# Attention denominators: one TensorE group for four steps in place of two, on rotating PSUM banks

## The reference, cut to what matters

```python
x = h_t                                            # [8, 1024, 256]
xn = layernorm(x)
# attention A: 8 heads, low-rank keys (c_kv) and queries (c_q), rotary part of 32
attnA = softmax(q @ k.T * (128 + 32) ** -0.5) @ v_c
# attention B: 16 heads of 16; tokens fall in two classes by a cosine with g_info;
# a token attends to its own class (and 5 register tokens, which average both)
attnB = softmax(where(mask, q * 16 ** -0.5 @ k.T, -inf)) @ v
out = x + attnA @ W_O + b_O + attnB @ W_proj + b_proj
```

## Time and profile before

| | |
|---|---|
| median of 3 runs | 3112.72 us (3109.84 to 3118.35) |
| the profiled execution | 3124.31 us, its span 3122.5 us |
| busy: TensorE, VectorE, ScalarE, GpSimd | 2950.3, 2243.7, 1738.0, 896.3 us |
| denominators' matmuls on TensorE | 135.1 us busy, 1024 records |
| additions on GpSimd | 585.3 us busy, 128 instructions |

### The profile page before, as it was taken

How to read it: one execution, slowest core, us unless ns; L and a number is a source line. 1 busy time by engine, 2 the same in 40 slices (tenths; PEclk the granted TensorE clock), 3 DMA queues, 4 the chain that set the end, 5 groups by cost and what they waited for, 6 DMA issues and landing times.

```text
span 3122.5 us, 45726 instructions
## 1 busy us (share of the span) xinstructions
PE 2950.3 (94%) x17346; PEld 1304.0 (42%) x17346; DVE 2243.7 (72%) x4016; ACT 1738.0 (56%) x2047; POOL 896.3 (29%) x359
## 2 busy tenths in 40 slices
PE   7899989999999999999999999999999999999997
PEld 5555533334433344344433443344333443344333
DVE  5566625798669866887678767986688767876791
ACT  2333345665457645665566555764566556654574
POOL 3322226102530054004500252016400450035201
PEclk9999989999999999999999999999999999999998
DMA  5755354225011420234021501152023402160001
GB/s 195 229 204 186 136 162 73 56 47 109 19 35 47 80 61 23 62 59 85 20 65 37 107 20 45 37 90 57 20 61 56 86 19 68 35 109 17 20 14 36
DMA packets 128411, 225.01 MB, mean 72 GB/s; under 512 B 48546, under 2 KB 79170, under 8 KB 126000
## 3 DMA queue, kind: packets, MB, share of 16 engines
q1 hardware_dynamic: 128192, 222.10, 29.4%
HBM read 143.44 MB, written 78.32 MB: 71 GB/s over the span
## 4 chain that ended last, share of the span: by engine, by line
PE 71%; DVE 22%; issue 2%; ACT 2%; DMA 2%; POOL 1%; SPq 1%; POOLq 0%; ACTq 0%; DVEq 0%
PE O L1209 22%; DVE mx L1502 18%; PE M L1128 14%; PE M L1122 8%; PE S L1188 5%; PE S L1191 4%; PE M L1225 4%; PE M L1080 3%; PE M L1168 2%; PE M L1170 2%; PE M L1141 1%; PE M L1098 1%; ACT PT L975 1%; PE M L1094 1%; POOL SUM L846 1%
## 5 line engine op out<-in xcount | busy, mean ns | idle before, releaser
L1502 DVE TENSOR_REDUCE mx<-M 128x1 f32<-128x512 f32 x3037 | 1940.2, 684 | 535.3 <-PE M L1128 334.7
L975 ACT ACTIVATE PTx<-S 128x1024 f32<-128x1024 f32 x768 | 746.3, 1022 | 504.1 <-PE S L1191 289.0
L975 ACT ACTIVATE PT<-S 128x1024 f32<-128x1024 f32 x768 | 748.0, 1022 | 472.2 <-PE S L1191 240.4
L1128 PE MATMUL M<-KB,QB 50*128 50x512 f32 x2048 | 726.3, 487 | 73.0 <-DVE mx L1502 44.3
L1128 PEld LDWEIGHTS M<-KB,QB 50*128 50x128 f32 x2048 | 295.8, 186 | 780.2 <-DVE mx L1502 571.6
L1191 PE MATMUL S<-QB,KB 52*128 52x512 f32 x2048 | 454.1, 417 | 2.5 <-ACT PT L975 1.6
L1122 PE MATMUL M<-KA,QA 98*128 98x512 f32 x989 | 414.2, 460 | 15.7 <-DVE mx L1502 10.0
L846 POOL TENSOR_TENSOR SUM<-PT 128x2048 f32<-128x2048 f32 x64 | 292.8, 4574 | 397.7 <-PE M L1225 184.0
L846 POOL TENSOR_TENSOR SUM<-PTx 128x2048 f32<-128x2048 f32 x64 | 292.5, 4570 | 177.2 <-PE M L1225 177.2
L1188 PE MATMUL S<-QA,KA 114*128 114x512 f32 x1024 | 318.8, 415 | 3.8 <-DMA QA<-sh_d 3.4
L1122 PEld LDWEIGHTS M<-KA,QA 98*128 98x128 f32 x989 | 168.3, 188 | 308.4 <-issue 179.3
(11 more groups left out here) (199 smaller groups left out, 1887.4 us busy)
## 6 DMA issues: line engine op xcount, KB each, us to landing
KA<-kt_d SPq DMA_DIRECT2D x48, 512.0 KB, 7.1
QB<-qk_d SPq DMA_DIRECT2D x192, 128.0 KB
KB<-qk_d SPq DMA_DIRECT2D x192, 128.0 KB
qk_d<-QB SPq DMA_DIRECT2D x16, 1024.0 KB, 4.1
kt_d<-QB SPq DMA_DIRECT2D x16, 1024.0 KB, 4.3
RB<-recb_d SPq DMA_DIRECT2D x64, 256.0 KB
vb_d<-VB SPq DMA_DIRECT2D x8, 1536.0 KB, 5.5
VB<-vb_d SPq DMA_DIRECT2D x8, 1536.0 KB, 12.7
```

What stands on the lines that cost most here:

```text
L975: nc.scalar.activation(probs(k)[:, 2 * pair:2 * pair + 2, :], Sg[pair][:, :].rearrange("p (j s) -> p j s", j=2), ACT.Exp, scale=SCALE_A if ...
L1128: done = mm(m[:, :], QB[rows, 2 * q + a, at:at + P], KB[rows, 2 * q + a, keys], start=True, stop=True)
L1502: v.tensor_reduce(mx[:, g % 2, unit, kh:kh + 1], m[:, :], AX.X, ALU.max).then_inc(free, 1)
```

## The change

- GpSimd adds four steps' exponentials in place of two: `add_four` is called for t = 1, 2, 3; the first call adds two steps into one of two `SUM` buffers, the second and third add one more step each in place. That is three additions for four steps, and not two. The second and third wait for the one before.
- TensorE has one denominators group for four steps, as a job `dn` at the end of step 4i+7 (the last one of a stage at step 3 of B). It isn't accumulated over a head group: each goes to its own bank, in turn with the other jobs, and ScalarE copies it to a half of `DEN` (`take_dens`, at every fourth step).
- `DN` is gone, so jobs take turns on three banks in all steps but the `rv` ones of B.
- SP moves both halves of a head group (`den_d` with one dimension more, `RC` too), and VectorE adds the halves before the reciprocal, which stands at step 7 of the next group in place of 5.
- The last `po` jobs stand at steps 13 to 16 and not 12 to 15. `load_residual(b, 1)` moves to the end of the B stage, ahead of `recs` of group 6 and behind the store of the first half, and the residual addition to the end of GpSimd's B stage.

```diff
-PAIRS = STEPS_A // 2
+QUADS = STEPS_A // 4
...
+    s[3][3].append(("dn", QUADS - 1))
...
+    for i in range(QUADS - 1):
+        s[4 * i + 7][3].append(("dn", i))
     if not first:
-        for c, at in enumerate((12, 13, 14, 15)):
+        for c, at in enumerate((13, 14, 15, 16)):
...
-        of = 3 if three is not None and k >= three and not RV_AT <= k < RV_AT + NC // 2 else 2
+        of = 2 if len(slots) == STEPS_B and RV_AT <= k < RV_AT + NC // 2 else 3
...
-    SUM = sb("SUM", [P, 4, HALF])
+    SUM = sb("SUM", [P, 2, 4, HALF])
+    DEN = sb("DEN", [P, 2, HALF])
...
             if kind == "a":
-                wait_apart(sp, dn_free, n * GA + (g + 1))
-                src = RB[0:P:32, slot, :]
+                for i in (2 * g, 2 * g + 1):
+                    spot = dn_spot(n, i)
+                    wait_apart(sp, m_free[spot.bank], spot.upto())
+                sp.dma_start(den_d[slot].rearrange("w h s -> h w s"), DEN[0:P:32, :, :]).then_inc(den_out, 16)
+                wait_apart(sp, den_out, at * 16 + 16)
+                sp.dma_start(RC[:, slot, :, :], den_d[slot].rearrange("w h (r c) -> (h r) w c", c=16)
+                             ).then_inc(rc_in, 16)
...
             for g in range(GA):
-                if before and g == 0:
-                    load_residual(b, 1)
...
                     store_out(b, 0, [b_spot(b, last, ("po", c)) for c in range(4)])
-                    if last:
-                        load_residual(b, 1)
+                    load_residual(b, 1)
...
+        def add_four(n, i, t):
+
+            k, done = 4 * i + t, n * (3 * QUADS) + 3 * i
+            four = SUM[:, i % 2]
+            if t == 1:
+                if n or i >= 2:
+                    spot = dn_spot(n, i - 2) if i >= 2 else dn_spot(n - 1, QUADS - 2 + i)
+                    wait_apart(pool, m_full[spot.bank], spot.upto())
+            else:
+                wait_apart(pool, summed, done + t - 1)
             wait_apart(pool, e_done, n * (2 * STEPS) + (2 * k + 2))
-            nc.gpsimd.tensor_tensor(SUM[:, :, :], probs(k - 1), probs(k), ALU.add).then_inc(summed, 1)
+            nc.gpsimd.tensor_tensor(four, probs(k - 1) if t == 1 else four, probs(k), ALU.add).then_inc(summed, 1)
...
-            for i in range(PAIRS):
-                g, at = i // 4, i % 4
-                add_pair(n, i)
+            for i in range(QUADS):
+                add_four(n, i, 1)
+                if i % 2 == 0:
+                    if i >= 4:
+                        scale(n, "a", i // 2 - 2)
                     elif before:
-                        scale(b, "b", GB - 2 + g)
-                if before and i == 1:
-                    residual(b, 1)
+                        scale(b, "b", GB - 2 + i // 2)
+                add_four(n, i, 2)
+                add_four(n, i, 3)
...
+            residual(b, 1)
...
                 if 4 <= k < STEPS_A + 4:
-                    act.wait_ge(summed, n * PAIRS + ((k - 4) // 2 + 1))
+                    j = k - 4
+                    act.wait_ge(summed, n * (3 * QUADS) + (3 * (j // 4) + max(0, j % 4 - 1) + 1))
...
-            act.wait_ge(dn_done, n * PAIRS + 4 * (g + 1))
+            act.wait_ge(m_full[spot.bank], spot.upto())
+            nc.scalar.activation(DEN[:, i % 2, :], M4[spot.bank][:, :], ACT.Copy).then_inc(m_free[spot.bank], 1)
...
+            elif kind == "dn":
+                i = j[1]
+                pe.wait_ge(summed, n * (3 * QUADS) + (3 * i + 3))
+                for jj in range(4):
+                    done = mm(m[32 * jj:32 * jj + 32, :], ones32[:, :], SUM[:, i % 2, jj, :], start=True, stop=True,
+                              skip_group_check=True)
...
-                if k >= 3 and k % 2 == 1:
-                    denominators(n, b, (k - 3) // 2)
...
-            v.reciprocal(RC[:, g % 2, :], RC[:, g % 2, :]).then_inc(rc_done, 1)
+            of = RC[:, g % 2, 0, :]
+            if kind == "a":
+                own.link(v.tensor_tensor(of, of, RC[:, g % 2, 1, :], ALU.add))
+                own.settle()
+            v.reciprocal(of, of).then_inc(rc_done, 1)
```

More of the change, by code:

```diff
@@ L175, in jobs_a, with banks @@
     return s
-def banks(slots, three):
+def banks(slots):
     out = []
     for k, step in enumerate(slots):
-        of = 3 if three is not None and k >= three and not RV_AT <= k < RV_AT + NC // 2 else 2
+        of = 2 if len(slots) == STEPS_B and RV_AT <= k < RV_AT + NC // 2 else 3
         out += [(j, of) for part in step for j in part if j[0] != "rv" or j[1] == 0]
@@ L208 @@
 JOBS_B, JOBS_LAST = jobs_b(True), jobs_b(False)
-AT_A0, R0 = index(banks(JOBS_A0, None), U_PASS)
-AT_B, U_B = index(banks(JOBS_B, THREE), R0)
-AT_A, U_A = index(banks(JOBS_A, None), U_B)
+AT_A0, R0 = index(banks(JOBS_A0), U_PASS)
+AT_B, U_B = index(banks(JOBS_B), R0)
+AT_A, U_A = index(banks(JOBS_A), U_B)
 LOOP = less(U_A, R0)
 R1 = tuple(x + (B - 1) * y for x, y in zip(R0, LOOP))
-AT_LAST, U_LAST = index(banks(JOBS_LAST, THREE), R1)
-AT_TAIL, _ = index([(j, 2) for j in TAIL], U_LAST)
+AT_LAST, U_LAST = index(banks(JOBS_LAST), R1)
+AT_TAIL, _ = index([(j, 3) for j in TAIL], U_LAST)
 class Spot:
@@ L900, in _ @@
         b_steps(B - 1, True)
-        residual(B - 1, 1)
         scale(B - 1, "b", GB - 2)
@@ L993, in take_out, with take_dens @@
                 nc.scalar.activation(OB[:, q // 2, cols], O[:, :], ACT.Copy).then_inc(o_free, 1)
-        def take_dens(n, g):
-            act.wait_ge(dn_done, n * PAIRS + 4 * (g + 1))
-            if not (n == 0 and g < 2):
-                act.wait_ge(o_done, n * GROUPS + (g - 1))
-            nc.scalar.activation(RB[:, g % 2, :], DN[:, :], ACT.Copy).then_inc(dn_free, 1)
+        def take_dens(n, i):
+            spot, at = dn_spot(n, i), n * GROUPS + i // 2
+            if i % 2 == 0 and (n or i):
+                last = at - 1 if i else (n - 1) * GROUPS + (GA - 1)
+                act.wait_ge(den_out, last * 16 + 16)
+            act.wait_ge(m_full[spot.bank], spot.upto())
+            nc.scalar.activation(DEN[:, i % 2, :], M4[spot.bank][:, :], ACT.Copy).then_inc(m_free[spot.bank], 1)
         def a_steps(n, b, before):
@@ L1008, in a_steps @@
                     take_out(n, "a", k // NC - 1)
-                if k > NC and k % NC == 1:
-                    take_dens(n, k // NC - 1)
+                if k >= 7 and k % 4 == 3:
+                    take_dens(n, (k - 7) // 4)
         def b_steps(b, last):
@@ L1018, in b_steps @@
                     take_out(b, "b", k // NC - 1)
[L1019 to L1020 removed]
+                if k == 3:
+                    take_dens(b, QUADS - 1)
                 if k in (RS_AT, RS_AT + 1):
@@ L1106, in job @@
                 pass
-            elif spot.bank == 2 and spot.fixed in (R0[2], R1[2]):
-                pe.wait_ge(dn_free, b * GA + GA)
             elif not (spot.b is None and spot.fixed == 0):
@@ L1211, in values @@
             last.then_inc(pv_done, 1)
-        def denominators(n, b, i):
-            g, c = i // 4, i % 4
-            if c == 0:
-                if g == 0 and b is not None:
-                    pe.wait_ge(m_free[2], b * LOOP[2] + U_B[2])
-                elif g == 0:
-                    pe.wait_ge(m_free[2], U_PASS[2])
-                else:
-                    pe.wait_ge(dn_free, n * GA + g)
-            pe.wait_ge(summed, n * PAIRS + (i + 1))
-            for jj in range(4):
-                last = mm(DN[32 * jj:32 * jj + 32, :], ones32[:, :], SUM[:, jj, :],
-                          start=(c == 0), stop=(c == 3), skip_group_check=True)
-            last.then_inc(dn_done, 1)
         def of_batch(j, n, b):
-            own = j[0] in ("mb", "rs", "rt", "rv", "po") or (j[0] == "fa" and j[1] == "b")
+            own = j[0] in ("mb", "dn", "rs", "rt", "rv", "po") or (j[0] == "fa" and j[1] == "b")
             return b if own else n
@@ L1296, in b_steps @@
                     values(b, STEPS_A - 1, "a")
-                if k == 1:
-                    denominators(b, b, PAIRS - 1)
                 some(k, 3)
@@ L1494, in job @@
             kind = j[0]
-            if kind in ("rs", "rt") or (kind == "rv" and j[1] + 1 < NC):
+            if kind in ("dn", "rs", "rt") or (kind == "rv" and j[1] + 1 < NC):
                 return
@@ L1570, in a_steps @@
                     job(j, a_spot(n, b, j), b if j[0] == "po" else n, b)
-                if k % NC == 5:
-                    if k >= NC:
-                        invert(n, "a", k // NC - 1)
-                    elif before:
-                        invert(b, "b", GB - 1)
+                if k == 5 and before:
+                    invert(b, "b", GB - 1)
+                if k >= 15 and k % NC == 7:
+                    invert(n, "a", k // NC - 1)
         def b_steps(b, last):
@@ L1589, in b_steps @@
                     registers(b, last, k - RX_AT)
-                if k % NC == 5:
-                    invert(b, *(("b", k // NC - 1) if k >= NC else ("a", GA - 1)))
+                if k == 7:
+                    invert(b, "a", GA - 1)
```

(4 more changed lines are left out.)

38 lines of the change are left out of this document (15 added, 23 removed).

## The result

| | before | after |
|---|---|---|
| median | 3112.8 us (3109.8 to 3118.4) | 3079.3 us (3076.9 to 3086.7) |
| profiled execution: its span | 3122.5 us | 3084.9 us |
| busy: TensorE, VectorE, ScalarE, GpSimd | 2950.3, 2243.7, 1738.0, 896.3 us | 2881.6, 2302.6, 1750.9, 1185.5 us |

The ratio is 0.9894, 95% interval 0.9871 to 0.9917: faster by 1.1%. The forecast was 3011 us, with 2975 to 3075 as its range, so about a third of the forecast gain came and the time lies just over the range. In the profiles the gain is 37.6 us of span, where 102 were forecast; some of it is scatter, since the profiled execution before took 3124.3 us, 11.5 over its median.

What follows compares the result with a forecast made beforehand. TensorE bounds the A stages now, GpSimd after: stretch 119.8 + 2.5 + 1 = 123.3 us against 137.6, about 100 over seven stages, plus 2 in the first. 102 off the median gives 3011 us; own range 2990 to 3035, wider range 2975 to 3075.

Steps and rivals of the forecast that it cites:

- The rest at nothing: Small edits, among them eight ScalarE copies and four VectorE additions a stage, cost nothing, covered by idle time.
- if that cover went: Bound should ScalarE's and VectorE's idle time not hide the small copies and additions: 6.6 us a stage.
- the paragraph on contention: VectorE's four new additions could hold GpSimd up, at most 2.7 us a stage, giving 3030; no sign seen in trace.
- GpSimd takes TensorE's place as the bound: In A stages, 24 additions of 4.57 us, hand-overs and scalings sum to 119.8 us on GpSimd, against TensorE's 119.
- stretch: From an A stage's first addition to the exponential of step 35, in the next B stage: 137.6 us before, 123.3 forecast.
- TensorE's savings: In the stretch, fewer denominators groups save 7.7 us, the third bank 3 and 7: TensorE alone 119 us, 112 to 129.
- The moved residual: Loading XR behind the output store starts an A stage's first addition 2.5 us late, bounds 0 and 8.
- The first stage: First A stage, which ends on loads for the B stage: gain 2 us, bounds 0 and 6.
- The clock rival: TensorE idles a fifth of the time in second halves, its clock falls, half the gain is lost: 3061 us, chance 0.12.
- The loads late: XR comes 8 us late and not 2.5, so a stage gains 8.8 us: 3049 us, chance 0.12.
- No change: GpSimd's in-place addition with hand-over costs 5.2 us, not 4.6 to 4.85, taking 14 us a stage; chance 0.05.
- Slower: The clock stays down in the A stages' second halves, the stretch becomes 141 us: 3135 us, chance 0.08.

Runs made afterwards that it cites:

- reduction kernel: The changed kernel with VectorE adding the two halves by a one-operand tensor_reduce in place of the two-operand addition: 3023.5 us, 0.9716.
- control: The kernel before with an unused one-operand reduction of 16 columns ahead of each of A's 32 reciprocals on VectorE: 3116.0 us, 0.9997.

## Why the prediction was wrong, and what of it was right

| span of the profiled execution, difference to before | forecast | after | reduction kernel |
|---|---|---|---|
| seven later stages, steps 0 to 36 | -100 | 7 x (141.3 - 149.3) = -56.0 | 7 x (134.4 - 149.3) = -104.3 |
| first stage | -2 | +9.4 | +2.7 |
| before the first stage | 0 | +2.8 | +2.7 |
| all else | 0 | +6.2 | -0.9 |
| sum | -102 | -37.6 | -99.8 |

The table is of single executions, and that of the kernel before was a long one. In the control's trace, which is the same kernel with 32 cheap reductions more, steps 0 to 36 take 147.8 us and not 149.3, so some 10 us of both gains are scatter: by the medians they are 33.5 and 89. That of the reduction kernel is 12 us short of the 102 forecast.

**The step that failed** is "The rest at nothing", its "Four 128x16 additions on VectorE, each under a maximum's 0.68 us". Each of the three in a stage takes up to 3.66 us. Their work is 0.17 us; the rest is the GpSimd instruction that happens to run. The miss is the price of a single term: the reduction in its place brings the kernel from 3079.3 to 3023.5 us. That is 56 us of the 68 between forecast and result. The bound given, 6.6 us a stage "if that cover went", was for all small edits together and would have been 46 us; it was kept out of the sum, because the rows had no addition of two SBUF operands on VectorE and the nearest row that was taken, a maximum, reads one, from PSUM. That 6.6 lies so near to the 6.9 us a stage that the holds cost (141.3 - 134.4) is luck: it counts a length of 0.68 us for each addition, and more than half of it is ScalarE's copies.

The forecast came close to it, in the paragraph on contention, and took the wrong side: it let GpSimd be held up for the length of VectorE's short instruction, and found no sign of it in GpSimd's lengths. Those do stay at 4.57 us: it is the short instruction that waits for the long one. The trace of the kernel before has no sign of it either: in the stages no VectorE instruction with two operands in SBUF stands beside a GpSimd one, and the 12 of the first pass that stand beside a GpSimd `tensor_scalar` aren't held, as shown below. The Trainium skill (SBUF — State Buffer, Who interferes with whom) says that a VectorE instruction with two SBUF inputs and a GpSimd instruction that reads SBUF exclude each other, whoever issued first holding the shared ports for its whole length, and that one SBUF input doesn't contend. The traces agree for GpSimd's additions, and on the single input: the hold ends 0.03 to 0.04 us behind the addition, and the reduction's 0.19 us never grew. A GpSimd instruction held by VectorE is in none of these runs. By that rule the price could have been had from a row of the kernel before, as an estimate: up to 4.57 us each, 2.3 us in the mean, three times a stage (2.7 measured).

For another GpSimd instruction that reads SBUF the traces don't bear the rule out. In the first pass of the kernel before, a VectorE product of two operands in SBUF stands wholly inside a GpSimd `tensor_scalar`, which has one tensor to read (timelines of GpSimd and VectorE):

```profile
136.64 1.22 POOL L813 TENSOR_SCALAR PTx<-PT,early 128x256 f32<-128x256 f32 x1
...
137.02 0.45 DVE L1405 TENSOR_TENSOR early<-early 128x256 f32<-128x256 f32 x1
```

The twelve traces have 144 such VectorE instructions that start while a `tensor_scalar` runs. None of them takes over 0.47 us, and 0.40 to 0.43 is what their kind takes with GpSimd idle; the 96 that are held in these runs all stand beside an addition of two operands. Whether GpSimd's second operand, its operation or its length makes the difference was not tried.

**GpSimd takes TensorE's place as the bound: right.** 24 additions of 4.57 us, hand-overs of 0.27 us, the additions of a stage over 119.1 us after the first starts in the reduction kernel (119.8 forecast). Shortening the chain gave 63 us more, so it was the bound. With the later start the reduction kernel's stretch is 119.6 + 2.9 = 122.5 us, where 123.3 were forecast.

**TensorE's savings: right, a little low.** With most of GpSimd's third additions gone the forecast's stretch is 115.7 us (113.1 and 2.6 of later start), where 119 were summed for TensorE. Steps 0 to 36 take 127.9 us there with three banks, and 144.0 with two and all additions. The bank is thus worth up to 16 us a stage to TensorE, where 10 were summed ("bounds 0 and 7" and "0 and 10"), and 9.6 to the kernel, since GpSimd stops it there. The denominators' 7.7 us were not tried alone; nearest to it is the kernel with two banks, 4 us a stage under the control (144.0 and 147.8), the later start included.

**The moved residual: right** in time (sum 3 us late, 2.5 forecast) and in sign. It is no gain either way: 2.4 us of GpSimd in the stage or ahead of it.

**The first stage: wrong**, -2 forecast and +9.4 measured. The loads were named, but the step read their effect off the end of the stage ("the stage ends on them") and not off the small transfers in the same queue, of which `DEN` is now one and blocks ScalarE. The bounds, 0 and 6, had no loss in them. In the reduction kernel 2.7 us of loss are left; spread loads turn it into a gain of 5.

**The clock rival: right in what happens, not in why.** Its fall does come in the later halves, but behind the 2.7 us for which the held VectorE kept TensorE waiting. The mean granted clock is 0.977 before, 0.962 after and 0.981 with the reduction, where GpSimd is the bound just as well; over steps 0 to 36 of the seven later stages it is 0.981, 0.948 and 0.986. So "TensorE will idle there for a fifth of the time" isn't what brings it down. How much of the 56 us is the wait itself and how much the clock behind it was not separated: the held additions of the 24 places sum to 66 us, most of the first two of each stage under GpSimd's chain, and both went together in every run.

**The other rivals.** The loads late (3049), by 8 us: no, 3 us. No change (3113), on additions of over 5.2 us: no. Slower (3135): no. The rise before the first stage, 2.8 us, is within what the traces differ by: the first exponential of the stage starts at 427.2 to 430.2 us in the twelve of them, and at 429.1 and 429.2 in the two that add an instruction to the kernel before. The 6 us in the B stages of the changed kernel were not traced further; they are gone with the reduction.

Of what was to show it: GpSimd over 90% busy, idle 0.27 us, exponentials released by SUM and the residual last before the stage, all seen. TensorE busy near 85%: no, 94% in batch 1's stage, partly at the low clock, and 96% in the reduction kernel, as a busy TensorE includes matmuls stretched by their waits. "VectorE waiting for RC" was listed as a sign of trouble; it was the right tile, but the trouble stood in the busy time of its instruction and in no wait.

## What to carry to other kernels

Before a small operation is put on VectorE beside long GpSimd additions of two operands, count its operands in SBUF. With two of them it costs up to the longest GpSimd instruction and not its own length; with one in PSUM, or written as a reduction over both halves, it costs what it should. Ask then where each hold falls: one that another engine's chain covers costs little, one at the end of that chain costs more than its length. When an engine has a group whose mean is far above its shortest, compare the end of each with the end of what runs on the engine beside it: a wait of this kind shows as busy time, and neither the waits nor the idle column has it.

Where a move makes a queue's small transfer feed a copy that stands in the order of the exponentials, price the loads that stand ahead of it in the queue.

## What the runs showed of the hardware that was not expected

- VectorE's 128x16 addition of two SBUF operands takes 0.17 us with GpSimd idle and up to 3.66 us (3.79 in the kernel before with such additions) with a 4.57 us addition running; it ends 0.03 to 0.04 us after that one. It slips in between two GpSimd instructions that follow each other at once. GpSimd's instructions keep their length.
- A `tensor_reduce` of the same data (0.19 us) and an addition with one operand in PSUM (0.43 us) are not held. Nor is a VectorE `tensor_tensor` of 128x256 with both operands in SBUF beside a GpSimd `tensor_scalar` of 1.22 us (144 cases, 0.47 us at most).
- Two GpSimd additions of 128x1024 take 0.14 us more than one of 128x2048 (4.71 against 4.57), so splitting a long one is a cheap way to let VectorE in: 26 us of the 56 by the medians.
- A TensorE that was busy for 0.72 of 3 us had its clock at 0.50 in the next 3. A stop of 2.7 us like this one stands at the third hold of five of the seven later stages, and steps 32 to 36 are 5.2 us longer in the mean than without the holds: the stop and the low clock together.
